# Last edge layer of a graph network: sums and expansions cut into pieces between the halves of the gathers, and four signals of TensorE for nine

## The chip, the cores and the metric

The kernel runs on one core of a Trainium2 chip. Its engines are TensorE (PE, matrix products into PSUM), VectorE (DVE), ScalarE (ACT), GpSimd (POOL, which issues the indirect DMAs here) and SyncE (SP, which issues the plain loads). The metric is the time of one execution on the device in microseconds.

## The reference, cut to what matters

A graph with 6250 nodes of 16 features and 206250 edges, sorted by their target node, goes through four graph layers. The change touches only the fourth, in which every edge has one of 90 relation types:

```python
def _L3_gnn_ref(h, he, Ws, Wa, weight, w_comp, src, dst, rel_type):
    W_rel = jnp.matmul(w_comp, V).reshape(num_rels, in_dim, out_dim)   # 90 matrices of 16 x 16
    h_src = h[src]
    e = jnp.concatenate([h_src @ Ws.T, he @ Ws.T, h[dst] @ Ws.T], axis=1) @ Wa.T
    msg = jnp.einsum('ei,eio->eo', h_src, W_rel[rel_type]) * e
    return jax.ops.segment_sum(msg, dst, num_segments=n_nodes)

h = jnp.maximum(_layernorm(x, axis=-1), 0.0)
x = x + _L3_gnn_ref(h, edge_attr_16, ..., src, dst, edge_type_90)
```

So each edge fetches its source node's row, multiplies it by the matrix of its type, weighs it by a scalar, and is added into its target's row.

## The kernel before, in words

`relation_layer` (from line 2043) does this layer in groups of 1024 edges: `SUP` = 8 tiles of 128 edges (`SE` = 1024), 202 groups k in all. A group is of one of three kinds (`kinds`). The first `PLAIN` = 11 are "plain": POOL fetches their source rows by indirect DMA, while TensorE makes a table with the product of every node and every type. The rest alternate nearly one to one. 96 are "table" groups: POOL fetches the finished products by indirect DMA (L2191, 8 per group, slots for `RT` = 12 groups). 95 are "matmul" groups: everything is computed on the engines. `EK` lists the plain and matmul groups, `GK` the table groups; iteration i of the loop stands for EK[i], and `after[i]` holds the table groups between it and the next.

The steps of a matmul group i:

- `make_hot` (L2194, DVE): after the keys were loaded by SP, 7 one-hot tiles of 1024 edges (L2206, L2207) and one of the types (`tyh`, L2211). Its buffer is one of two, so it waits for the last gather of group i - 2.
- `gather` (L2218, PE): for each half h of the edges (512) and each of two tables p, 7 matmuls of 128x512 into the PSUM bank `ps_g[p]` (L2225). Each set of seven gives a signal, and ACT evicts the bank with a relu into `sel` (L2231). The next set into the same bank waits for that eviction.
- `fold_rows` (L2233, PE): 16 small matmuls of 16 columns (L2240) turn the four `sel` tiles into the source rows in `ps_f`; they wait for the last eviction. `keep_rows` (ACT, L2248) copies them to `G`.
- `expand` (L2250, PE): 24 matmuls of 256 columns (L2260) put each edge's 16 x 16 matrix into the four banks `ps_w`; each bank waits for the product of the group before. Two signals, after 12 and after 24.
- `messages` (DVE): reads `G` (L2271), multiplies `ps_w` by `G` (L2288), reduces (L2280), and weighs (L2298). `make_dst` (L2216, DVE) makes the one-hots of the targets.
- `add_up` (L2306, PE): 8 fp32 products, 16 records in the profile (L2312), add a group's messages into a window of 64 nodes in one half of the bank `ps_a`. They wait for the messages and for the copy of the group two before. `put_sums` (ACT, L2323, L2326) copies the window out and stores it by DMA. A table group has the same two steps, after `weigh_rows` (L2303, L2304, DVE).

Iteration i issues, in this order for each engine: loads of keys (SP), fetches of table groups (POOL), `fold_rows(i-1)`, `keep_rows(i-1)`, `expand(i-1)`, the one-hots of i + 1 and the messages of i - 1 (DVE), both halves of `gather(i)`, `add_up` and `put_sums` of group EK[i-2], and the same for the table groups after it. Each engine works through its own list in order. The engines meet only through semaphores: `c.by(ins)` makes an instruction add to a counter and returns the value to wait for (L84). In a steady iteration TensorE gives 9 such signals: 4 of the gather, 1 of the fold, 2 of the expansion, 1 for each of the two sums. Who waits for the signal of a sum (`a_tok`): `put_sums` on ACT, `make_dst` and `messages` of a later group on DVE, and POOL, before it fetches the table group 12 later into the same slot. While plain groups run, one table tile (`table_tile`) stands in the middle of the expansion.

## Time and profile before

| | us |
|---|---|
| median of 3 runs | 4394.57 |
| lowest, highest | 4373.16, 4407.93 |
| profiled execution | 4357.18 |
| its span | 4353.5 |
| TensorE busy in the span | 3665.5 |

The span runs from the first to the last instruction of the program; the profiled execution is longer by what lies around it. The busy time of TensorE comes from matmuls that overlap and whose ends are modelled, so a busy TensorE isn't one at its peak. In the timeline, a row merges instructions of one kind; "idle before" is the time its engine stood, with what ended it. Names of tiles are shortened: `l_ps_g` is `ps_g`, `l_ps_x` is `ps_f` and `ps_a`, `ring` holds the one-hots, the products and the rows of table groups.

### The profile page before, as it was taken

The page shows a single profiled execution, that of the slowest core. Times are in us where ns is not written, and L with a number is a line of the kernel's source. Part 1 is how long each engine was busy: PE and PEld are TensorE (multiplying, and loading weights), DVE is VectorE, ACT ScalarE, POOL GpSimd, SP SyncE. Part 2 cuts the span into 40 slices and gives each one's busy share as a digit, 9 for nine tenths or more (in the row PEclk, how much of TensorE's full clock was granted, in tenths as well). Part 3 has the DMA queues.
Part 4 walks back from the last instruction along what each step waited for, and adds up shares of the span by engine and source line. Part 5 has one row for each costly group of instructions (what it writes and reads, how often), then busy time and mean ns, then how long its engine had stood idle before and what let it go on. Part 6 is the DMA issues. An engine that isn't in the chain of part 4 may idle for free. (4 is left out here: it accounts for less than half of the span.)

```text
span 4353.5 us, 77864 instructions
## 1 busy us (share of the span) xinstructions
PE 3665.5 (84%) x28548; PEld 2130.3 (49%) x28548; DVE 2710.6 (62%) x6415; ACT 1324.1 (30%) x2874; POOL 1900.8 (44%) x1856
## 2 busy tenths in 40 slices
PE   6787879999998768888889896672799989998998
PEld 4566645544554324444444443341455555555555
DVE  8999953222212546676666674442677767777777
ACT  6999930011000213332333331340122212222222
POOL 1000006830000466676667650267366666666650
PEclk8999989998999879898888997665799888888889
DMA  5444468662465412222222225771122222222221
GB/s 149 83 83 80 60 270 304 219 236 91 168 238 245 138 30 50 50 51 47 44 50 51 51 51 192 295 238 18 37 44 44 44 39 44 46 45 41 44 44 40
DMA packets 471195, 445.62 MB, mean 102 GB/s; under 512 B 357553, under 2 KB 406609, under 8 KB 459675
## 3 DMA queue, kind: packets, MB, share of 16 engines
q1 hardware_dynamic: 389178, 391.82, 29.1%
q0 software_dynamic: 55216, 38.70, 6.0%
q10 hardware_dynamic: 26417, 10.05, 0.9%
q8 instruction: 231, 3.78, 0.4%
q14 instruction: 153, 1.25, 0.1%
HBM read 346.18 MB, written 95.85 MB: 102 GB/s over the span
## 5 line engine op out<-in xcount | busy, mean ns | idle before, releaser
L1814 POOL DMA_INDIRECT rows<-typed_table,ring x640 | 754.4, 1179 | 368.1 <-issue 180.1
L2225 PE MATMUL l_ps_g<-ring,h_part 128*128 128x512 f16 x2660 | 641.8, 401 | 92.3 <-issue 81.3
L1408 PE MATMUL L_ps<-ring,L_T 128*128 128x448 fp8e4 (+1 forms) x4606 | 670.9, 382 | 45.6 <-DMA ring<-adj 42.1
L2191 POOL DMA_INDIRECT ring<-typed_table,l_idxA x384 | 397.1, 1034 | 275.8 <-PE l_ps_x L2312 163.9
L1408 PEld LDWEIGHTS L_ps<-ring,L_T 128*128 128x128 f16 (+1 forms) x4606 | 327.9, 104 | 375.8 <-issue 60.8
L2191 POOL DMA_INDIRECT l_rows<-typed_table,l_idxA x384 | 394.6, 1028 | 234.1 <-PE l_ps_x L2312 127.4
L2231 ACT ACTIVATE l_sel<-l_ps_g 128x512 f16<-128x512 f32 x380 | 226.1, 597 | 851.6 <-PE l_ps_g L2225 399.1
L2225 PEld LDWEIGHTS l_ps_g<-ring,h_part 128*128 128x128 f16 x2660 | 273.6, 103 | 431.4 <-issue 165.4
L620 PE MATMUL cells<-keys,lows 128*128 128x147 f16 (+5 forms) x2744 | 372.6, 283 | 121.6 <-DVE keys L581 105.9
L2206 DVE TENSOR_SCALAR ring<-l_krow,W 128x1024 f16<-128x1024 f16 x570 | 234.7, 483 | 302.9 <-remote 183.2
L2260 PE MATMUL l_ps_w<-rel,l_tyh 90*128 90x256 bf16 x2544 | 397.5, 327 | 19.1 <-DVE ring L2288 15.6
L1843 ACT ACTIVATE sel<-ps_g 128x512 f16<-128x512 f32 x488 | 263.3, 596 | 477.9 <-PE ps_g L1837 321.4
L1873 DVE TENSOR_TENSOR dinvB<-G,tyh 128x1024 f16<-128x1024 f16 x244 | 288.2, 1223 | 165.5 <-ACT G L1860 107.9
L1837 PE MATMUL ps_g<-ring_fifth,h_part 128*128 128x512 f16 x1464 | 365.8, 408 | 25.7 <-issue 25.0
L620 PEld LDWEIGHTS cells<-keys,lows 128*128 128x128 f16 x2744 | 286.7, 141 | 204.7 <-DVE keys L581 171.8
L1837 PE MATMUL ps_g<-dinvB,h_part 128*128 128x512 f16 x1464 | 370.0, 414 | 3.7 <-issue 3.3
L581 DVE TENSOR_SCALAR keys<-build_or_wx,offset 128x441 f16<-128x441 f16 (+3 forms) x1438 | 366.2, 332 | 0.0
L1420 DVE SCALAR_TENSOR_TENSOR L_Y<-L_ps,L_scale,dinvB 128x448 f32<-128x448 f32 x84 | 57.4, 684 | 493.9 <-PE L_ps L1408 493.6
L2260 PEld LDWEIGHTS l_ps_w<-rel,l_tyh 90*128 90x128 bf16 x2544 | 287.5, 116 | 100.4 <-issue 29.4
L698 ACT ACTIVATE ring<-cells 128x784 fp8e4<-128x784 f32 x392 | 326.1, 833 | 24.0 <-PE cells L620 23.6
L2288 DVE TENSOR_TENSOR ring<-l_ps_w,l_G 128x512 f32<-128x512 f32 x380 | 258.8, 683 | 46.0 <-remote 33.3
L2280 DVE TENSOR_REDUCE l_msg<-ring 128x32 f32<-128x512 f32 x424 | 278.3, 678 | 0.0
(369 smaller groups left out, 4466.4 us busy)
## 6 DMA issues: line engine op xcount, KB each, us to landing
ring<-adj SPq DMA_DIRECT2D x67, 2744.0 KB, 10.9
adj<-ring SPq DMA_DIRECT2D x14, 2744.0 KB, 9.1
typed_table<-ring SPq DMA_DIRECT2D x49, 765.0 KB
ring_fifth<-src_div_mod_rows SPq DMA_DIRECT2D x122, 256.0 KB
l_krow<-src_div_mod_rows SPq DMA_DIRECT2D x95, 256.0 KB
l_trow<-type_row SPq DMA_DIRECT2D x106, 180.0 KB
attr<-in_he POOLq DMA_DIRECT2D x25, 512.0 KB, 5.7
klast<-last_keys SPq DMA_DIRECT2D x81, 128.0 KB
```

What stands on the lines that cost most here:

```text
L581: ins = dve.tensor_scalar(keys[g % OB][:, j, 0:C], iotaC[:, 0:C], offset[g // BG % 2][:, g % BG, j:j + 1], HIT, ALU.is_equal, ALU.mult)
L620: ins = pe.matmul(to, lows[g // QG % 3][:, :, g % QG * KT + j], made[:, (a1 - a) * NT:(b1 - a) * NT], start=j == FIRST[h], stop=j == LAST[ ...
L698: act.activation(ring[c % RING][:, :, gl * GD:(gl + 1) * GD].rearrange("p k (h d) -> p k h d", h=2), cells[g % CB][:, :, 0:HD * NT].rearra ...
L1408: ins = pe.matmul(bank[at:at + rows, 0:CH], d["T"][q][:, k, 0:rows], ring[r][:, k, :], start=n < side, stop=n >= NT - side, tile_position= ...
L1814: r_tok_[g] = r_in[b].by(pool.indirect_dma_start(rows[b][:, j, :], None, t1_dram, bass.IndirectOffsetOnAxis(ap=idxA[:, k * SUP + j:k * SUP ...
L1837: ins = pe.matmul(ps_g[2 * h + p][:, 0:HE], parts[p][:, j, :], hot[b][:, j, h * HE:(h + 1) * HE], start=False, stop=j == GJ - 2)
L1843: selt[i, h] = c_sel.by(act.activation(sel[b][2 * h + p][:, :], ps_g[2 * h + p][:, 0:HE], ACT.Relu))
L1873: typed_tok[i] = c_typed.by(dve.tensor_tensor(typed[b][:, p, :, :, :], gp, ty, ALU.mult))
L2191: rt_tok[g] = r_in[b].by(pool.indirect_dma_start(table_rows[b][:, j, 0:RC], None, t3_dram, bass.IndirectOffsetOnAxis(ap=idxA[:, k * SUP + ...
L2225: ins = pe.matmul(ps_g[p][:, 0:HE], parts[p][:, j, :], hot[b][:, j, h * HE:(h + 1) * HE], start=j == 0, stop=j == GJ - 1)
L2260: ins = pe.matmul(ps_w[q][:, (j % 2) * 256:(j % 2 + 1) * 256], tyh[i % 3][:, j * P:(j + 1) * P], rel[:, p, :], start=p == 0, stop=p == 2)
L2280: return c_msg.by(dve.tensor_reduce(m[:, 2 * q:2 * q + 2, 0:F], prod[q], AX.X, ALU.add))
```

## The change

It moves work of the last layer on TensorE and lets tokens ride on other instructions' signals.

- `gather`: one signal for a half, after both banks; ACT waits once and evicts both.
- `expand` comes in two calls of 12 matmuls with one signal each; `fold_rows` stands between them and has no signal of its own: its token is that of the second half. `keep_rows` comes after it.
- `add_up` of the group EK[i-2] stands between the two halves of `gather(i)`; its token is that of the second half of the gather.
- The sums of the table groups stand after the gather as before, but have no signal; their token is that of the first half of the next iteration's expansion, and their `put_sums` comes there.

In iterations without a gather, and at the end, the sums keep signals of their own. A steady iteration has 4 signals of TensorE.

```diff
                         ins = pe.matmul(ps_g[p][:, 0:HE], parts[p][:, j, :], hot[b][:, j, h * HE:(h + 1) * HE],
                                         start=j == 0, stop=j == GJ - 1)
-                    gat[i, h] = c_gat.by(ins)
-                    act.wait_ge(*gat[i, h])
-                    if p == 0 and i >= 2 and by_matmul[i - 2]:
-                        act.wait_ge(*fold_tok[i - 2])
+                gat[i, h] = c_gat.by(ins)
+                act.wait_ge(*gat[i, h])
+                if i >= 2 and by_matmul[i - 2]:
+                    act.wait_ge(*fold_tok[i - 2])
+                for p in range(2):
                     selt[p, "sel"] = selt[i, h] = c_sel.by(act.activation(sel[b][2 * h + p][:, :], ps_g[p][:, 0:HE], ACT.Relu))
...
-                        ins = pe.matmul(ps_f[:, j * F:(j + 1) * F], sel[i % 2][2 * h + p][:, q * P:(q + 1) * P], fold[:, :], start=p == 0, stop=p == 1)
-                fold_tok[i] = c_fold.by(ins)
+                        pe.matmul(ps_f[:, j * F:(j + 1) * F], sel[i % 2][2 * h + p][:, q * P:(q + 1) * P], fold[:, :], start=p == 0, stop=p == 1)
...
-            def expand(i, between=()):
+            def expand(i, half):
                 pe.wait_ge(*ty_tok[i])
-                for q in range(SUP // 2):
-                    if q == SUP // 4:
-                        for m in between:
-                            table_tile(m)
+                for q in range(half * SUP // 4, (half + 1) * SUP // 4):
...
-                    if q % 2:
-                        w_tok[i, q - 1] = w_tok[i, q] = c_w.by(ins)
+                w_tok[i, q - 1] = w_tok[i, q] = c_w.by(ins)
+                if half == 1 and by_matmul[i]:
+                    fold_tok[i] = w_tok[i, q]
...
-                a_tok[k] = c_a.by(ins)
+                return ins
...
                 if 1 <= i <= n:
+                    expand(i - 1, 0)
+                    for k in unsignalled:
+                        a_tok[k] = w_tok[i - 1, 0]
+                        put_sums(k)
+                    unsignalled = []
                     if by_matmul[i - 1]:
                         fold_rows(i - 1)
+                    for m in tiles[ahead:ahead + 1]:
+                        table_tile(m)
+                    expand(i - 1, 1)
+                    if by_matmul[i - 1]:
                         keep_rows(i - 1)
-                    expand(i - 1, tiles[ahead:ahead + 1])
...
-                if i < n and by_matmul[i]:
+                gathers = i < n and by_matmul[i]
+                if gathers:
                     gather(i, 0)
+                if i >= 2:
+                    k = EK[i - 2]
+                    summed = add_up(k, dstP[(i - 2) % 3], msg[(i - 2) % 3], 2 * F, msg_tok[i - 2], dst_tok[i - 2])
+                if gathers:
                     gather(i, 1)
                 if i >= 2:
-                    k = EK[i - 2]
-                    add_up(k, dstP[(i - 2) % 3], msg[(i - 2) % 3], 2 * F, msg_tok[i - 2], dst_tok[i - 2])
+                    a_tok[k] = gat[i, 1] if gathers else c_a.by(summed)
                     put_sums(k)
                     for g in after[i - 2]:
                         k = GK[g]
-                        add_up(k, dstG[g % 4], table_rows[g % RT], MC, rows_tok[g], dstg_tok[g])
-                        put_sums(k)
+                        summed = add_up(k, dstG[g % 4], table_rows[g % RT], MC, rows_tok[g], dstg_tok[g])
+                        if i < n:
+                            unsignalled.append(k)
+                        else:
+                            a_tok[k] = c_a.by(summed)
+                            put_sums(k)
```

## Rows read from the trace of the kernel before

**Rows 1.** Page: busy time over the span, and the clock in 40 slices

```profile
PE 3665.5 (84%) x28548; PEld 2130.3 (49%) x28548; DVE 2710.6 (62%) x6415; ACT 1324.1 (30%) x2874; POOL 1900.8 (44%) x1856
...
PEclk8999989998999879898888997665799888888889
```

**Rows 2.** Windows: length, busy us (count) by engine, clock, DMA share, GB/s

```profile
3210.00:3320.00 110.00, 97.07 (x855) 60.98 (x852) 87.02 (x200) 26.70 (x60) 68.90 (x68) 1.00 0.23 44
...
4241.00:4338.00 97.00, 92.71 (x875) 62.28 (x873) 80.73 (x186) 25.38 (x61) 0.00 (x0) 0.98 0.10 24
3606.40:3621.70 15.30, 13.74 (x102) 8.51 (x101) 11.87 (x28) 3.05 (x7) 10.31 (x11) 0.84 0.34 56
3621.70:3633.60 11.90, 11.90 (x103) 7.42 (x101) 9.16 (x22) 3.05 (x7) 6.29 (x7) 0.92 0.21 32
...
3100.00:4338.00 1238.00, 1141.43 (x9194) 712.89 (x9192) 952.87 (x2184) 276.99 (x642) 697.31 (x672) 0.89 0.22 42
```

**Rows 3.** Timeline of PE, an iteration near the end: start, length, instructions

```profile
4261.85 6.21 PE L2225 MATMUL l_ps_g<-ring,h_part 128*128 128x512 f16 x28
4267.99 0.94 PE L2312 MATMUL l_ps_x<-l_msg,ring 128*64 128x32 f32 x13
...
4269.77 0.56 PE L2240 MATMUL l_ps_x<-fold,l_sel 128*128 128x16 f16 x16
4270.18 2.78 PE L2260 MATMUL l_ps_w<-rel,l_tyh 90*128 90x256 bf16 x24
4272.80 0.60 PE L2225 MATMUL l_ps_g<-ring,h_part 128*128 128x512 f16 x2
```

**Rows 4.** Timeline of ACT, the same iteration

```profile
4268.10 0.60 ACT L2231 ACTIVATE l_sel<-l_ps_g 128x512 f16<-128x512 f32 x1 [0.91 <-PE l_ps_g L2225]
...
4271.61 0.28 ACT L2248 ACTIVATE l_G<-l_ps_x 128x128 f32<-128x128 f32 x1 [0.78 <-ACT l_sums L2323]
```

**Rows 5.** Timeline of DVE, the same iteration

```profile
4267.48 0.29 DVE L2304 TENSOR_TENSOR ring<-ring,l_eG 128x128 f32<-128x128 f32 x1
4268.17 2.47 DVE L2206 TENSOR_SCALAR ring<-l_krow,W 128x1024 f16<-128x1024 f16 x6 [0.40 <-PE l_ps_g L2225]
...
4271.34 0.67 DVE L2216 TENSOR_TENSOR ring<-iota,dloc 128x512 f32<-128x512 f32 x1
4271.94 0.27 DVE L2271 TENSOR_TENSOR l_ua<-l_G,t_u 128x128 f32<-128x128 f32 x1
```

**Rows 6.** Timeline of PE, a long iteration in the middle

```profile
3606.41 6.21 PE L2225 MATMUL l_ps_g<-ring,h_part 128*128 128x512 f16 x28
...
3614.15 0.33 PE L2312 MATMUL l_ps_x<-ring 128*64 128x33 f32 x3 [0.22 <-issue]
3615.55 0.42 PE L2312 MATMUL l_ps_x<-ring 128*64 128x33 f32 x5 [1.06 <-issue]
3616.24 0.56 PE L2240 MATMUL l_ps_x<-fold,l_sel 128*128 128x16 f16 x16 [0.27 <-ACT l_sel L2231]
...
3616.66 5.28 PE L2260 MATMUL l_ps_w<-rel,l_tyh 90*128 90x256 bf16 x24
```

**Rows 7.** Timeline of ACT, the same long iteration

```profile
3608.13 0.60 ACT L2231 ACTIVATE l_sel<-l_ps_g 128x512 f16<-128x512 f32 x1 [2.61 <-PE l_ps_g L2225]
3609.64 0.60 ACT L2231 ACTIVATE l_sel<-l_ps_g 128x512 f16<-128x512 f32 x1 [0.91 <-issue]
3614.13 0.60 ACT L2231 ACTIVATE l_sel<-l_ps_g 128x512 f16<-128x512 f32 x1 [3.90 <-PE l_ps_g L2225]
3615.59 0.60 ACT L2231 ACTIVATE l_sel<-l_ps_g 128x512 f16<-128x512 f32 x1 [0.86 <-remote]
```

**Rows 8.** Groups of TensorE, 3100 to 4338: busy us, mean ns, idle before

```profile
L2240 PE MATMUL l_ps_x<-fold,l_sel 128*128 128x16 f16 x1456 | 53.3, 170 | 25.5 <-issue 15.6 <-ACT l_sel L2231 9.6
```

More of the change, by code:

```diff
@@ L2352, in relation_layer @@
                 if 1 <= i <= n:
+                    expand(i - 1, 0)
+                    for k in unsignalled:
+                        a_tok[k] = w_tok[i - 1, 0]
+                        put_sums(k)
+                    unsignalled = []
                     if by_matmul[i - 1]:
                         fold_rows(i - 1)
+                    for m in tiles[ahead:ahead + 1]:
+                        table_tile(m)
+                    expand(i - 1, 1)
+                    if by_matmul[i - 1]:
                         keep_rows(i - 1)
-                    expand(i - 1, tiles[ahead:ahead + 1])
                 if i >= 2:
```

## The prediction

> **What bounds it now.** I read the page first, then busy time by stretches, then the order of time on one engine at a time. The page's slices place the change: it touches only the last edge layer, about the last third of the span, where the clock row stays at 8 to 9 tenths for the most part [rows 1]. From 3100 to 4338 us, where gathers run, TensorE is busy 1141 of 1238 us and VectorE 953: TensorE is the bound, VectorE next, and POOL and ScalarE are not near [rows 2]. Count iterations by matmuls: one with gather, expansion, fold and both sums has 28 + 24 + 16 + 32 = 100 records, so 9194 are 92 iterations (the code has 95, the first of them earlier), 13.47 us each. An iteration at its best is seen near the end, when POOL has nothing more to fetch: from one gather's start to the next 4272.80 - 4261.85 = 10.95 us, without an idle gap [rows 3]. So 92 x (13.47 - 10.95) = 231 us of this layer are above its own best pace. Where they go is in a pair of neighbouring iterations that repeats (3606.4 to 3633.6): 15.3 us, then 11.9 us, at granted clocks of 0.84 and 0.92, that is, with some of the time at the 1.2 GHz level [rows 2].
>
> The long one shows how it is lost. The 28 gather matmuls take 6.21 us as they do at best [rows 3, 6]. But ScalarE, which should get one bank of four every 1.5 us (4268.10 is 6.25 after the gather's start) [rows 4], evicts the third at 3614.13, 7.7 us after the start, and the fourth at 3615.59, 9.2 us after it [rows 7]. The signals came about 3 us late. TensorE went on into the sums, then stood 0.22, 1.06 and, before the fold, 0.27 us for ScalarE [rows 6]; after that the expansion runs at half rate, 5.28 us for 24 against 2.78 [rows 3, 6]. The clock fell right after that idle. Near 3210 to 3320 the clock was full (1.00), yet 855 matmuls in 110 us are 12.87 us an iteration, so late signals cost without the clock falling too [rows 2]. No row tells why signals are late; with POOL idle (0.00 from 4241) they are not.
>
> **The change, part by part.** All sums are against the profiled execution, 4353.5 us of span and 4357.18 in all; the median of the three runs is 37.4 above that, and I add differences to the median.
>
> *Work on TensorE*: the same 100 matmuls, moved. Removed 0, added 0.
>
> *Nine signals to four* (four banks to two, fold, and both sums ride on others; two of the expansion stay). In the clean iteration the expansion's 24 matmuls with their two signals take 4272.80 - 4270.18 = 2.62 us, 109 ns each, and nothing stands behind a signal [rows 3]. Price 0; between 0 and, were a third of the 0.30 us of idle in front of such pieces due to signals, -9 us. I take 0. The Trainium skill (TensorE: Matmul & The Clock Gate, "The cost: per-tile semaphore tail") has increments that follow each other closely serialize at some 26 ns apiece; five fewer on 95 iterations would by that be an estimated 12 us, and the sum 12 us lower. The rows agree with none of it, as these signals lie microseconds apart.
>
> *More pieces.* Before: gather, two sums, fold, expansion. After: half expansion, fold, half expansion, half gather, sum, half gather, sum. 28 gathers at the pace inside the piece would be 6.04 us, and the sums start 6.14 after the gather did: a switch costs about 0.10 [rows 3]. There are up to three more per iteration: 0 to 0.30 us x 95 = 0 to +28; I take one, +10, since fold to expansion shows none.
>
> *Fold behind half an expansion.* Fold waits for ScalarE's last eviction. Over the layer TensorE stood 25.5 us before the fold, 9.6 of it put to ScalarE [rows 8]. Now the second sum and 12 expansion matmuls (1.3 us at full clock) run first, so that both evictions (2 x 0.60 after the signal) are covered even for a late signal. Gain 9.6 to 25.5; I take 20. What was late next in that place is nothing: the expansion waits for VectorE's products, done before.
>
> *Evictions after the pair.* The half's two relus start after 14 matmuls instead of 7 and 7. The next half's first bank needs the first relu, 0.03 + 0.60 us after the signal [rows 4]. The first sum, 16 of the 32 matmuls that take 1.78 us with their switch, about 0.9 us [rows 3], covers it with 0.3 us to spare. Price 0; without that cover 0.63 x 95 = +60.
>
> *ScalarE's and VectorE's order.* G is kept after the whole expansion instead of just after the fold, though before it stood behind two evictions of sums anyway: 4271.61, 1.84 us after the fold began [rows 3, 4]. Afterwards it comes at gather's end + 1.0 (switch and sum) + 2.6 + 0.4 (expansion, fold) + 0.3 and 0.3 (signal, the copy itself), so 4.6 us; VectorE is ready for it 3.8 us after it starts the one-hots at the gather's end (4268.17 to 4271.94) [rows 5]. So VectorE first stands 0.8 us. Its own work is 10.55 us of 10.95, with 0.40 of idle in front of the one-hots [rows 5]; it then starts its next round up to 0.4 us after the gather, finds G in time, and TensorE takes nothing from it sooner than a whole round later. Price 0, bound +0.4 x 95 = +38. At half clock G comes 2.5 us later still (5.28 against 2.78), but that pair gives VectorE 27.2 - 2 x 10.55 = 6 us of slack. The puts of sums and their DMAs are as many as before; the second sum's leaves ScalarE and frees POOL's slot half an expansion, some 1.3 us, later. POOL fetches 12 groups ahead, is busy 697 of 1238 us [rows 2] and waits for slots anyway: 0. SyncE's key loads and the plain part's table tiles keep their places: 0.
>
> Sum: +10 - 20 = -10 us, bounds -35 to +95 with every cover lost. 4394.57 - 10 = **4385**.
>
> **The rivals.** With a layer that has two regimes, these count for more than the sum.
>
> *A, the clock no longer falls.* The low-work stretch (two sums and fold, 2.2 us, lengthened by the idle) is cut up, so that the stretch of 3210 to 3320 becomes the rule: 92 x (13.47 - 12.87) = -55 us, 4340. For it: the clock fell right behind such a stretch [rows 6]. Against: 4241 to 4338 has the same uncut stretch at 0.98 clock, so the late signals, not the order, make it fall. 0.22.
>
> *B, the late signals go as well*, for fewer signals or a different rhythm: 10.95 + 0.15 us an iteration, 92 x 2.37 = -218, 4177. For it: such iterations exist; against it: those seen in number have an idle POOL, which the change doesn't give. 0.13.
>
> *C, slower: a late signal now hits between the halves.* The second half may not start before the first half's relu, and only 0.3 us is spare, where before every bank had the other bank's 1.5 us. If the signal of half 0 comes 3 us late, TensorE stands 2.7 us. If the lateness moves there, it replaces 0.22 + 1.06 + 0.27 = 1.55 us of idle [rows 6]: 46 long iterations x 1.15 = +53. If it comes at both, 46 x 2.7 = +124. Between them +88, 4483. It decides from 0.3 us of lateness on. For: between 3 us late evictions nothing in the trace binds them to the second half for good. Against: in the iteration read here the second is evicted at 3609.64, 3.2 us after the start, on time [rows 7]. 0.15.
>
> *D, slower: a fall in every iteration.* If the extra switches leave small gaps, the clock may fall each time, and every iteration takes 15.3: 92 x 1.83 = +168, 4563. The full clock from 4241 with four pieces speaks against it. 0.05. The Trainium skill has such a rule (TensorE: Matmul & The Clock Gate, "A second HAM failure mode: psum-queue depth-cycling"): short idles between groups of matmuls on cycling banks make the clock swing. What the trace has behind the 3616 idle agrees, the clean tail doesn't.
>
> *E, the change does nothing*, as when POOL or something outside paces the pair of iterations at 27.2 us: 4395. 0.05.
>
> **How the numbers follow.** The forecast has 0.40, spread 4350 to 4430. A measurement of this kernel tells about 1%, 44 us, from no change. Faster by more: A, B and little else, 0.36. Slower: C, D and an edge of the forecast with covers lost, 0.22. Within: 0.42. The range leaves out most of B and D, and reaches from between A and B to C: 4270 to 4485. The forecast's own range is 4350 to 4430.
>
> **What would show it.** In the profile after: (1) before the fold no idle on ScalarE, or this term is wrong; (2) from gather half to sum and back steps of 0.1 us; (3) ScalarE's relus in pairs, the first half's 0.03 us after its last matmul's end; (4) VectorE before L2271 up to 0.8 us idle and TensorE none for it; (5) long and short iterations alternating as before, 13.5 us on average: 12.9 says A, 11.1 B, over 14.3 C, 15.3 D. TensorE standing before the second half for ScalarE would make the prediction wrong upward, a granted clock above 0.95 downward.

## The result, and the profile after

The change made the kernel slower. Over 20 runs of each the median is 4414.43 us after (4366.08 to 4447.0) against 4374.65 before (4335.08 to 4413.82): a ratio of 1.0101, with an interval of 1.0072 to 1.0129, or some 44 us. (This ratio and those in the table below leave out executions more than 1.5% above the fastest of the same kernel, so they can differ a little from the ratio of the medians.) The forecast was 10 us faster; measured is 31 to 56 us slower. The time still lies inside the stated range, because that range reached far to both sides. The profiled execution took 4409.81 us with a span of 4405.7 (before 4357.18 and 4353.5).

In the changed kernel the gather is L2225 as before, its relu L2232, the fold L2241, the copy of G L2248, the expansion L2257, the sums L2310, their copies L2321, and the first read of G L2269. The page of the kernel after, first TensorE's clock, which hardly differs from [rows 1]:

```profile
PE 3665.5 (83%) x28548; PEld 2117.1 (48%) x28548; DVE 2716.7 (62%) x6415; ACT 1298.2 (29%) x2874; POOL 1905.9 (43%) x1856
...
PEclk8999989999998689889999997665998979998988
```

The same windows as in [rows 2], of after (window, its length, busy us and count of PE, PEld, DVE, ACT, POOL, granted clock, DMA share, GB/s):

```profile
3100.00:4380.00 1280.00, 1161.48 (x9217) 708.17 (x9214) 962.46 (x2196) 255.90 (x645) 709.94 (x672) 0.91 0.22 41
4285.00:4380.00 95.00, 94.11 (x844) 61.30 (x842) 81.33 (x185) 23.39 (x60) 0.00 (x0) 1.00 0.14 29
...
3200.00:4200.00 1000.00, 900.99 (x7079) 547.41 (x7078) 741.84 (x1694) 195.81 (x496) 611.75 (x578) 0.90 0.23 42
```

and the stretch 3200 to 4200 of before:

```profile
3200.00:4200.00 1000.00, 919.67 (x7301) 570.97 (x7300) 765.04 (x1753) 221.93 (x513) 619.74 (x598) 0.89 0.23 44
```

At 100 matmuls an iteration, 1000 us hold 73.01 iterations of before, 13.70 us each, and 70.79 of after, 14.13 us each. 0.43 us over the 95 iterations is 41 us, about the whole loss, at a clock that is no lower. (The two profiled executions differ by 52 us; from the layer's first expansion to its last matmul it is 43, and 8 lie before it, where nothing was changed.) Of the 0.43 us, 0.13 is more busy time of TensorE (12.60 against 12.73 us an iteration) and 0.30 is more idle time (1.10 against 1.40).

An iteration at its best, near the end where POOL is idle, shows the new order. The timeline of TensorE after (start, length, instructions):

```profile
4308.91 3.19 PE L2225 MATMUL l_ps_g<-ring,h_part 128*128 128x512 f16 x14
4312.02 1.12 PE L2310 MATMUL l_ps_x<-l_msg,ring 128*64 128x32 f32 x16
4313.07 3.19 PE L2225 MATMUL l_ps_g<-ring,h_part 128*128 128x512 f16 x14
4316.20 1.12 PE L2310 MATMUL l_ps_x<-ring 128*64 128x33 f32 x16
4317.25 1.48 PE L2257 MATMUL l_ps_w<-rel,l_tyh 90*128 90x256 bf16 x12
4318.57 0.55 PE L2241 MATMUL l_ps_x<-fold,l_sel 128*128 128x16 f16 x16
4318.98 1.47 PE L2257 MATMUL l_ps_w<-rel,l_tyh 90*128 90x256 bf16 x12
4320.28 1.89 PE L2225 MATMUL l_ps_g<-ring,h_part 128*128 128x512 f16 x8
```

From one gather to the next it is 4320.28 - 4308.91 = 11.37 us, without an idle gap, where before took 10.95 [rows 3]. By pieces, from start to start: gather 3.11 + 3.13 = 6.24 against 6.14 (+0.10); sums 1.05 + 1.05 = 2.10 against 1.78 (+0.32); expansion 1.32 + 1.30 = 2.62 against 2.62; fold 0.41 against 0.41. ScalarE and VectorE in the same iteration:

```profile
4312.13 1.09 ACT L2232 ACTIVATE l_sel<-l_ps_g 128x512 f16<-128x512 f32 x2 [2.75 <-PE l_ps_g L2225]
4316.31 1.09 ACT L2232 ACTIVATE l_sel<-l_ps_g 128x512 f16<-128x512 f32 x2 [3.09 <-PE l_ps_g L2225]
...
4320.48 0.28 ACT L2248 ACTIVATE l_G<-l_ps_x 128x128 f32<-128x128 f32 x1 [1.39 <-PE l_ps_w L2257]
```

```profile
4320.79 0.29 DVE L2269 TENSOR_TENSOR l_ua<-l_G,t_u 128x128 f32<-128x128 f32 x1 [0.57 <-ACT l_G L2248]
```

The relus come in pairs, and the second pair (4316.31) is done under the sum and half an expansion. VectorE stands 0.57 us for G, and nothing on TensorE waits for it.

In the middle of the layer the late signals are there as before ([rows 6, 7]). TensorE, ScalarE and VectorE in such an iteration of after:

```profile
3712.71 1.12 PE L2310 MATMUL l_ps_x<-l_msg,ring 128*64 128x32 f32 x16
3714.91 3.18 PE L2225 MATMUL l_ps_g<-ring,h_part 128*128 128x512 f16 x14 [1.08 <-issue]
3718.03 0.71 PE L2310 MATMUL l_ps_x<-l_rows,ring 128*64 128x33 f32 x9
3719.13 0.19 PE L2310 MATMUL l_ps_x<-l_rows,ring 128*64 128x33 f32 x1 [0.40 <-issue]
3719.84 0.53 PE L2310 MATMUL l_ps_x<-l_rows,ring 128*64 128x33 f32 x6 [0.52 <-issue]
```

```profile
3714.17 1.09 ACT L2232 ACTIVATE l_sel<-l_ps_g 128x512 f16<-128x512 f32 x2 [2.68 <-PE l_ps_g L2225]
3720.03 1.08 ACT L2232 ACTIVATE l_sel<-l_ps_g 128x512 f16<-128x512 f32 x2 [4.78 <-remote]
```

```profile
3720.11 2.46 DVE L2206 TENSOR_SCALAR ring<-l_krow,W 128x1024 f16<-128x1024 f16 x6 [1.80 <-remote]
```

The first half of this gather ended at 3712.8, its relu began 1.4 us later, and the second half of the gather began 1.08 us after the sum, at 3714.91, just behind the first relu (3714.17 + 0.60); the profile puts that idle to no wait. The second half ended at 3718.1 and its relus began at 3720.03.

A signal is "late" here against the end of a matmul, and those ends are modelled. What is late is on TensorE's side and not ScalarE's reception: VectorE, which waits for the same signal before it makes new one-hots, starts 0.08 us after ScalarE. In the long iteration of before it is the same, 3615.59 on ScalarE [rows 7] and on VectorE

```profile
3615.66 2.47 DVE L2206 TENSOR_SCALAR ring<-l_krow,W 128x1024 f16<-128x1024 f16 x6 [3.33 <-remote]
```

And TensorE itself stands inside a sum then, where the program has no wait between the 16 matmuls: 1.06 us in [rows 6], until 3615.55, and 0.40 and 0.52 us in the rows of after, until 3719.84. Whether its matmuls or only its signals are held up, and by what, no row tells. Counted over 3200 to 4200, VectorE waits 65 times before the one-hots in both kernels; 34 of these waits in before and 55 in after end more than 0.3 us behind the gather's last matmul, by 3.0 and 2.7 us in the median. So the change did not make late signals rarer.

Over the layer (3100 to 4380, groups of TensorE and one of VectorE: count, busy us, mean ns, idle before):

```profile
L2225 PE MATMUL l_ps_g<-ring,h_part 128*128 128x512 f16 x2561 | 640.0, 406 | 39.7 <-issue 33.5 <-ACT l_sel L2232 6.2
L2257 PE MATMUL l_ps_w<-rel,l_tyh 90*128 90x256 bf16 x2208 | 318.6, 298 | 19.5 <-issue 19.3
...
L2241 PE MATMUL l_ps_x<-fold,l_sel 128*128 128x16 f16 x1472 | 53.6, 171 | 39.9 <-ACT l_sel L2232 31.5 <-issue 8.2
```

```profile
L2269 DVE TENSOR_TENSOR l_ua<-l_G,t_u 128x128 f32<-128x128 f32 x92 | 26.8, 291 | 74.7 <-ACT l_G L2248 42.2 <-issue 32.5
```

The first and the last of them in before, 3100 to 4338:

```profile
L2225 PE MATMUL l_ps_g<-ring,h_part 128*128 128x512 f16 x2530 | 604.3, 398 | 23.1 <-issue 12.1 <-ACT l_sel L2231 11.0
```

```profile
L2271 DVE TENSOR_TENSOR l_ua<-l_G,t_u 128x128 f32<-128x128 f32 x91 | 25.4, 279 | 27.8 <-ACT l_G L2248 15.7 <-issue 11.9
```

The idle before the fold did not go away, it rose from 25.5 us [rows 8] to 39.9; that before the gathers rose from 23.1 to 39.7, and the expansion, which never stood before, stands 19.5 us. The sums stand less, 18.5 us for 46.7.

### The profile page after: what moved, and what is told of

The parts are those of the page before. It is cut to its first block and busy times, and to the rows that moved or that the text cites. A ratio compares the mean times of both kernels' runs of the same rounds, so it can differ in the third digit from the quotient of the medians.

```text
span 4405.7 us, 77969 instructions
## 1 busy us (share of the span) xinstructions
PE 3665.5 (83%) x28548; PEld 2117.1 (48%) x28548; DVE 2716.7 (62%) x6415; ACT 1298.2 (29%) x2874; POOL 1905.9 (43%) x1856
## 5 line engine op out<-in xcount | busy, mean ns | idle before, releaser
L2225 PE MATMUL l_ps_g<-ring,h_part 128*128 128x512 f16 x2660 | 671.1, 408 | 85.7 <-issue 79.1
L2225 PEld LDWEIGHTS l_ps_g<-ring,h_part 128*128 128x128 f16 x2660 | 269.1, 104 | 414.4 <-issue 172.2
L2232 ACT ACTIVATE l_sel<-l_ps_g 128x512 f16<-128x512 f32 x380 | 206.2, 595 | 845.5 <-remote 415.4
L2257 PE MATMUL l_ps_w<-rel,l_tyh 90*128 90x256 bf16 x2544 | 383.0, 306 | 47.6 <-issue 39.2
L1837 PE MATMUL ps_g<-ring_fifth,h_part 128*128 128x512 f16 x1464 | 356.2, 401 | 19.2 <-issue 18.5
L2257 PEld LDWEIGHTS l_ps_w<-rel,l_tyh 90*128 90x128 bf16 x2544 | 259.0, 108 | 120.6 <-issue 66.8
```

Of the source, the lines that this page charges most:

```text
L1837: ins = pe.matmul(ps_g[2 * h + p][:, 0:HE], parts[p][:, j, :], hot[b][:, j, h * HE:(h + 1) * HE], start=False, stop=j == GJ - 2)
L2225: ins = pe.matmul(ps_g[p][:, 0:HE], parts[p][:, j, :], hot[b][:, j, h * HE:(h + 1) * HE], start=j == 0, stop=j == GJ - 1)
L2257: ins = pe.matmul(ps_w[q][:, (j % 2) * 256:(j % 2 + 1) * 256], tyh[i % 3][:, j * P:(j + 1) * P], rel[:, p, :], start=p == 0, stop=p == 2)
```

## The experiments

Five groups ran, each on one chip beside runs of the kernel before. The chips turned out to be of two kinds. On chips 2 and 13 hardly a signal of TensorE comes late (none of 75 such waits in e1 and of 68 in e2, 3 of 71 in k0) and before takes about 3780 us; on chips 9, 14 and 4, and in the runs of the result above, about half of them or more come late, by 1.6 to 3.7 us in the median, and before takes 4375 to 4469. Each ratio is against before on the same chip; "us per iteration" is the window's length by its matmuls over 100 (900 us from 2800 on chips 2 and 13, else 1000 us from 3200).

| run | chip | median us | before | ratio (95%) | us per iteration | clock |
|---|---|---|---|---|---|---|
| e1_sum_between | 2 | 3797.64 | 3778.34 | 1.0056 (1.0034 to 1.0079) | 11.35 | 1.00 |
| e2_fold_between | 2 | 3784.66 | 3778.34 | 1.0011 (0.9988 to 1.0033) | 10.93 | 1.00 |
| e3_five_signals | 2 | 3848.83 | 3778.34 | 1.0190 (1.0154 to 1.0226) | 11.89 | 1.00 |
| e4_sums_together | 2 | 3847.17 | 3778.34 | 1.0183 (1.0150 to 1.0216) | 11.83 | 1.00 |
| a0_after | 9 | 4513.43 | 4468.78 | 1.0126 (1.0051 to 1.0200) | 14.70 | 0.89 |
| b0_before | 9 | 4445.18 | 4468.78 | 0.9950 (0.9899 to 1.0001) | 14.09 | 0.87 |
| e8_after_nine | 9 | 4382.99 | 4468.78 | 0.9833 (0.9766 to 0.9899) | 13.29 | 0.95 |
| e5_before_no_fetch | 9 | 4198.08 | 4468.78 | 0.9422 (0.9311 to 0.9533) | 11.46 | 0.99 |
| f1_gather_signals | 14 | 4388.40 | 4392.16 | 0.9987 (0.9944 to 1.0031) | 14.04 | 0.90 |
| f2_other_signals | 14 | 4321.21 | 4392.16 | 0.9852 (0.9794 to 0.9911) | 13.27 | 0.96 |
| g1_fold_between | 14 | 4374.65 | 4392.16 | 0.9969 (0.9932 to 1.0005) | 13.67 | 0.90 |
| g2_sum_between | 14 | 4363.01 | 4392.16 | 0.9957 (0.9921 to 0.9993) | 13.68 | 0.91 |
| k0_after | 13 | 3798.09 | 3781.07 | 1.0052 (1.0031 to 1.0073) | 11.36 | 1.00 |
| k1_sum_signals | 13 | 3798.09 | 3781.07 | 1.0051 (1.0027 to 1.0075) | 11.37 | 1.00 |
| k2_fold_signal | 13 | 3790.62 | 3781.07 | 1.0042 (1.0016 to 1.0067) | 11.36 | 1.00 |
| k3_pool_later | 13 | 3794.63 | 3781.07 | 1.0035 (1.0014 to 1.0056) | 11.35 | 1.00 |
| m1_sum_signals | 4 | 4465.06 | 4462.62 | 0.9979 (0.9940 to 1.0018) | 14.13 | 0.92 |
| m3_pool_later | 4 | 4446.97 | 4462.62 | 0.9964 (0.9932 to 0.9997) | 13.97 | 0.91 |

### One part of the order at a time

**e1_sum_between** is the kernel before, with its nine signals, and only the sum of EK[i-2] moved between the halves of the gather.

```diff
                 if i < n and by_matmul[i]:
                     gather(i, 0)
-                    gather(i, 1)
                 if i >= 2:
                     add_up(k, dstP[(i - 2) % 3], msg[(i - 2) % 3], ...)
+                if i < n and by_matmul[i]:
+                    gather(i, 1)
```

> Of the change only this: the sum of group EK[i-2] stands between the two halves of the gather; fold, expansion and all nine signals as before. Theory S (switches): in the kernel after, an iteration at its best takes 11.38 us instead of 10.95, all of it because two sums that stood together took 1.78 us and now take 1.05 each, and the gather in two pieces takes 6.25 instead of 6.14. Then this kernel has a best iteration of 11.38 us too, and costs 92 x 0.43 = +40 us, about as much as the whole change (+1.0%). Theory L (late signals): what costs is that TensorE stands more for ScalarE, mostly before the fold, which here is where it was; then this is +0 to +15 us. Theory N (number of signals matters): nine signals kept, the switches' cost without the gain from fewer signals, over +1.0%.

**e2_fold_between** is the kernel before with only the fold moved between the halves of the expansion.

```diff
+                    expand(i - 1, 0)
                     if by_matmul[i - 1]:
                         fold_rows(i - 1)
                         keep_rows(i - 1)
-                    expand(i - 1, tiles[ahead:ahead + 1])
+                    for m in tiles[ahead:ahead + 1]:
+                        table_tile(m)
+                    expand(i - 1, 1)
```

> Of the change only this: the fold stands between the two halves of the expansion, with its own signal, and G is kept right after it. Theory S: a piece of expansion more costs nothing (1.32 + 0.40 + 1.31 us in the kernel after against 0.41 + 2.62), best iteration 10.95, and the fold's idle of 25.5 us goes mostly: 0 to -20 us, no difference that can be told. Theory L: the idle before the fold grows as in the kernel after (39.9 us), +10 to +20 us.

The windows 2800 to 3700, of e1 and then of e2:

```profile
2800.00:3700.00 900.00, 900.00 (x7930) 580.97 (x7928) 827.91 (x1901) 240.94 (x555) 706.88 (x634) 1.00 0.28 53
```

```profile
2800.00:3700.00 900.00, 900.00 (x8237) 586.94 (x8236) 863.23 (x1976) 250.79 (x577) 700.68 (x655) 1.00 0.29 54
```

No idle in either, at full clock; e2 keeps the pace of before (10.93 against the 10.95 of [rows 3]), e1 is at 11.35. In the iteration Theory S holds: moving the one sum costs all of the 0.42 us, the split expansion nothing. Where it lies, on TensorE of e1 and of e2:

```profile
3306.90 3.19 PE L2225 MATMUL l_ps_g<-ring,h_part 128*128 128x512 f16 x14
3310.02 1.12 PE L2312 MATMUL l_ps_x<-l_msg,ring 128*64 128x32 f32 x16
3311.07 1.25 PE L2225 MATMUL l_ps_g<-ring,h_part 128*128 128x512 f16 x5
```

```profile
3309.04 0.94 PE L2309 MATMUL l_ps_x<-l_msg,ring 128*64 128x32 f32 x13
3309.76 0.24 PE L2309 MATMUL l_ps_x<-ring 128*64 128x33 f32 x1
...
3309.96 0.92 PE L2309 MATMUL l_ps_x<-ring 128*64 128x33 f32 x13
3310.82 1.38 PE L2257 MATMUL l_ps_w<-rel,l_tyh 90*128 90x256 bf16 x11
```

Side by side the sums run 13 matmuls in 0.72 us (55 ns each), then six records that alternate between the two in 0.20 us (33 ns each), then 13 in 0.86. Alone, 16 take 1.05 us. At 55 ns each 16 would be 0.89, so the end of a sum costs some 0.16 us, now twice, and the six that overlapped lose 6 x 22 ns = 0.13: 0.29 of the 0.32. The other 0.10 is the second start of a gather (14 x 216 ns = 3.02 of the 3.12 that a half takes). The Trainium skill (TensorE: Matmul & The Clock Gate, "Measured speedup vs the span model") has matmuls on different column tiles run in parallel, three of them 2.38 times as fast. Here two tiles (the two halves of `ps_a`) overlap only where the second sum follows the first, in six records of 32.

The whole program lost less than these iterations say: by medians e1 lost 19 us, not 0.42 x 95 = 40, and k0 below 17. In the two profiled executions the stretch from the first gather to the last is 43 us longer in e1 than in e2, but the median of e2 lies some 16 us above its profiled execution. Runs of before spread over 41 us, those of e1 over 16. Why the typical run of before and of e2 is slower than its own best pace there is open.

### Signals where none is late

**e3_five_signals** is the order of before with merged signals: one for each half of the gather, one for the two sums, the fold's on the expansion's. **e4_sums_together** is the kernel after with the plain sum moved back behind the gather, next to the table sum; both tokens are then that of the next half expansion.

```diff
# e3, against before
-                    gat[i, h] = c_gat.by(ins)
+                gat[i, h] = c_gat.by(ins)
...
-                fold_tok[i] = c_fold.by(ins)
+                        fold_tok[i - 1] = w_tok[i - 1, 0]
# e4, against after
                     gather(i, 0)
+                    gather(i, 1)
                 if i >= 2:
                     summed = add_up(k, dstP[(i - 2) % 3], ...)
-                if gathers:
-                    gather(i, 1)
```

> Order of the kernel before, but five signals for nine: one per half of the gather with both evictions behind it, the fold's token is that of the first half of the expansion, and two sums that stand together share one. Theory S: signals cost nothing, best iteration 10.95, within 0.3% of before. Theory N: fewer signals come late less often, mean iteration under 13.2 us, -20 us or more. Theory L: evictions in pairs make the next half wait for the relu (no sum covers it here): each iteration +0.63 us, best iteration 11.6, +58 us.

> The kernel after with one thing undone: the sum of EK[i-2] stands behind the whole gather again, next to the table group's sum, and both tokens are that of the next half expansion (4 signals). But now nothing covers the first relu between the halves: 0.63 us. Theory S: the sums take 1.78 together again and the gather 6.14; less 0.43 and, if the cover matters as I reckoned, plus 0.6: best iteration 11.0 if the relu is covered by something else, 11.6 if not. Total 0 us or +58 us against before. Theory L: as the kernel after, +44 us, whatever the order of the sums.

TensorE in e3:

```profile
3306.96 3.18 PE L2225 MATMUL l_ps_g<-ring,h_part 128*128 128x512 f16 x14 [0.78 <-ACT l_sel L2232]
```

Every second half stands 0.78 us for the relu of the first, 74.0 us in all, and e4 shows the same 0.78. Both lose 1.8 to 1.9%, about 70 us: that is the price of the pair of relus without its cover, which the prediction put at +60. In after the sum covers it, for 0.42 us.

**k0_after** is the changed kernel itself, **k1_sum_signals** gives the sums their signals back, **k2_fold_signal** the fold its own, and **k3_pool_later** has all nine, but POOL waits for the later token that it has in the changed kernel.

```diff
# k1, against after (add_up; put_sums again right behind it)
-                return ins
+                a_tok[k] = c_a.by(ins)
# k2, against after (fold_rows)
+                fold_tok[i] = c_fold.by(ins)
# k3, against the nine signals of e8 below
-                    pool.wait_ge(*a_tok[GK[g - RT]])
+                    at = next(x for x in range(n) if g - RT in after[x])
+                    pool.wait_ge(*w_tok[at + 2, 0])
```

> The kernel after, unchanged, as the measure for the three beside it on the same chip. With late signals +1.0 to +1.3% against before, without them +0.6 to +1.1%.

> The kernel after with both sums signalling for themselves again; the fold without a signal, the gather in pairs: six signals. Theory M1 (the sums' borrowed tokens cost, for the copies of sums and POOL's next fetch come later): as fast as with nine signals, 1.5% under before where signals come late. Theory M2 (the fold's borrowed token costs, for G comes half an expansion later): as the kernel after, +1%. Without late signals all three are within 0.3% of each other.

> The kernel after with the fold signalling for itself again; sums without signals, the gather in pairs: five signals. Theory M1: as the kernel after, +1%. Theory M2: 1.5% under before.

> The order of the kernel after with all nine signals (1.7% under before on a chip with late signals), but POOL waits for its free slot on the signal that it has in the kernel after, the next iteration's first half expansion, instead of the sum's own, some 1.4 us later. Theory Q (it is POOL's start, and where its fetches then fall on the gather, that makes the borrowed tokens costly): as slow as the kernel after, +1%. Rival A (it is ScalarE's copies of the sums, which come later or stand before G): stays 1.7% under before.

The window of k0:

```profile
2800.00:3700.00 900.00, 899.28 (x7924) 580.50 (x7923) 831.77 (x1901) 219.98 (x555) 707.30 (x633) 1.00 0.27 52
```

With four signals TensorE stood 0.72 us of 900, with nine (k3) not at all; all four kernels take 11.35 to 11.37 us an iteration, and their ratios lie within 0.17 points of each other, with intervals that overlap. Where hardly a signal is late, four or nine of them are the same, and the loss is that of the pieces alone. VectorE stands 46.5 us for G in these 900 us of k0, and TensorE has no idle for it.

### Where signals are late

**a0_after** and **b0_before** are the two kernels as they are, **e8_after_nine** is the order of after with every signal of before, and **e5_before_no_fetch** is the kernel before without POOL's fetches from the 13th table group on: their sums use the rows that lie in the slots.

```diff
# e8, against after
-                gat[i, h] = c_gat.by(ins)
+                    gat[i, h] = c_gat.by(ins)
...
+                fold_tok[i] = c_fold.by(ins)
...
-                return ins
+                a_tok[k] = c_a.by(ins)
# e5, against before
+                if g >= RT:
+                    rt_tok[g] = rt_tok[g - RT]
+                    return
```

> The kernel after, unchanged, beside the kernel before on whatever chip this is. Where the four kernels so far ran, no signal came late and each had one iteration time: 11.40 us with the sum between the halves, 10.94 with the fold between. Theory S (switches and the sums' lost overlap, 0.43 us an iteration): on a chip without late signals this kernel has 11.38 us in nearly every iteration, and is 20 to 43 us slower than before. On a chip with late signals both have 13 to 14 us and the same difference. Theory L (more idle for late signals): without late signals there is no difference.

> The kernel before, unchanged, to have its profile from the same chip. Theory S: 10.95 us in nearly every iteration if no signal comes late there; the last layer then ends some 240 us earlier after its first gather than in the trace of before. If the signals are late, 13.5 us as in the trace of before.

> The order of the kernel after with all nine signals of the kernel before (each bank of the gather, the fold and both sums signal for themselves, evictions per bank, G kept as after, behind the whole expansion). Theory S: signals cost nothing, iteration 11.38 to 11.40 us and the time of the kernel after within 0.3%. Theory N (five signals fewer gain something, 0.13 us an iteration or more): 11.5 us or more, 12 us slower than after.

> The kernel before without POOL's fetches for the table groups from the thirteenth on (their sums use the rows that lie in the slots), so that POOL is idle in most of the layer. Theory P (late signals come with POOL's fetches): on a chip where before has late signals, this one has none and 10.95 us an iteration. Rival (late signals are a state of the chip and of the load on TensorE alone): 13 us and more there too. On a chip without late signals both are 10.95.

The windows 3200 to 4200 of a0, b0, e8 and e5, in this order:

```profile
3200.00:4200.00 1000.00, 875.88 (x6805) 527.91 (x6803) 717.92 (x1638) 188.63 (x478) 592.65 (x562) 0.89 0.23 41
```

```profile
3200.00:4200.00 1000.00, 915.41 (x7097) 560.75 (x7096) 745.25 (x1707) 214.38 (x496) 604.92 (x584) 0.87 0.24 43
```

```profile
3200.00:4200.00 1000.00, 910.24 (x7527) 560.94 (x7526) 785.13 (x1806) 225.95 (x526) 665.37 (x616) 0.95 0.25 45
```

```profile
3200.00:4200.00 1000.00, 950.72 (x8725) 622.30 (x8723) 910.14 (x2091) 264.21 (x610) 0.00 (x0) 0.99 0.19 46
```

Three readings. Without the fetches the same program on the same chip goes from 14.09 to 11.46 us an iteration with a clock of 0.99, and late waits of VectorE go from 33 of 65 to 1 of 68: the late signals come with POOL's fetches (two executions of e5). Whether it is POOL's work or the traffic of its indirect DMAs is not told apart, and the same fetches do no harm on chips 2 and 13. The order alone, with nine signals, is a gain of 1.7% here (0.9766 to 0.9899): the clock rises from 0.87 to 0.95. It does not make the signals punctual, 61 of 71 waits are late in e8; it has work to do meanwhile. And merging the signals turns that into a loss of 1.3%: e8 to a0 is 4382.99 to 4513.43, 130 us or 3.0%. Theory S, the same +0.43 us as elsewhere (here a0 has +0.61 over b0) and e8 within 0.3% of after, failed. b0 is before against itself; its 0.5% says how much of a ratio on this chip is noise.

**f1_gather_signals** gives the changed kernel back only the four gather signals (six in all), **f2_other_signals** only those of the fold and the sums (seven), with the relus still in pairs. **g1_fold_between** and **g2_sum_between** are the edits of e2 and e1.

```diff
# f1, against after
-                gat[i, h] = c_gat.by(ins)
+                    gat[i, h] = c_gat.by(ins)
# f2, against after
+                fold_tok[i] = c_fold.by(ins)
...
-                return ins
+                a_tok[k] = c_a.by(ins)
```

> The kernel after with its gather signals undone: one signal and one eviction per bank (four again), while the fold and both sums still have none of their own; six signals. On the chip where signals come late, the kernel after took 14.5 us an iteration and its order with all nine signals 13.2. Theory E (evictions in pairs lengthen the path of a late signal: the fold then waits for two relus, 0.6 us more, and what the gather does next finds no bank free): this is as fast as with nine, 1.7% under before and 2.9% under after. Theory M (the merged tokens of fold and sums cost, as G, the copies of sums and POOL wait for a later signal): as the kernel after, +1%. On a chip without late signals both say +0.6 to +1.0% (11.38 us an iteration).

> The other half of it: the kernel after with signals of their own for the fold and both sums again, but one signal and paired evictions for each half of the gather; seven signals. Theory E: as slow as the kernel after, +1%. Theory M: as fast as with nine, 1.7% under before. Without late signals both +0.6 to +1.0%.

> The kernel before with only the fold between the halves of the expansion, nine signals, gather and sums whole, once more, hoping for a chip with late signals (on the one without it was 10.94 us an iteration, +0.1%). Theory C (what saved time in the order with nine signals is that work stands between the last, late eviction and the fold that needs it): a late signal is covered by half an expansion, 1.3 us: 92 x 0.6 to 1.3 = 55 to 120 us under before. Rival H (what saved it is the sum between the halves, which keeps the gather's halves apart): same as before.

> The kernel before with only the first sum between the halves of the gather, nine signals, once more (11.40 us an iteration and +0.56% on the chip without late signals). Theory C: the fold stands one sum closer to the gather's end, so a late signal is covered less: +0.43 + up to 0.9 us an iteration, +1 to +2.5%. Rival H: -1% or more where signals come late.

The windows of f1 and f2:

```profile
3200.00:4200.00 1000.00, 918.05 (x7125) 558.58 (x7124) 747.90 (x1708) 209.36 (x498) 612.43 (x584) 0.90 0.23 43
```

```profile
3200.00:4200.00 1000.00, 905.02 (x7533) 556.04 (x7531) 788.78 (x1806) 208.88 (x527) 661.13 (x616) 0.96 0.24 45
```

f2 is at the pace of e8 (13.27 and 13.29), as Theory M said. f1 is not (14.04), but it is not as slow as after either: its ratio lies 1.35 points above f2, on the same chip, and 1.1 to 1.4 points under those of after (1.0101 and 1.0126), so neither Theory E nor M has it. With the fold's and the sums' tokens on time, pairing the relus costs next to nothing. The merged tokens of fold and sums cost about half of what merging all costs, and the pairs the other half, on top of them.

Groups of TensorE, 3200 to 4200, of g1 and then of g2:

```profile
L2225 PE MATMUL l_ps_g<-ring,h_part 128*128 128x512 f16 x2044 | 495.3, 401 | 57.5 <-issue 40.7 <-ACT l_sel L2231 16.8
...
L2240 PE MATMUL l_ps_x<-fold,l_sel 128*128 128x16 f16 x1168 | 41.6, 172 | 0.0
```

```profile
L2225 PE MATMUL l_ps_g<-ring,h_part 128*128 128x512 f16 x2033 | 485.0, 392 | 1.9 <-ACT l_sel L2231 1.0 <-issue 0.9
...
L2240 PE MATMUL l_ps_x<-fold,l_sel 128*128 128x16 f16 x1168 | 41.2, 171 | 77.8 <-ACT l_sel L2231 77.8
```

In g1 the fold, behind half an expansion, never stands; the idle is before the gathers instead, 57.5 us. In g2 the gathers never stand, covered by the sum, and the fold does, 77.8. By their ratios each alone gains 0.3 to 0.4%, which is no more than b0 differed from itself and far from what either theory gave, with the idle moved to the place that is still uncovered; both together gain 1.5% on the same chip (f2) and 1.7% on chip 9 (e8).

**m1_sum_signals** and **m3_pool_later** are the edits of k1 and k3 on a chip with late signals.

> The kernel after with both sums signalling for themselves again (fold without a signal, gather in pairs), once more, for a chip with late signals. There the kernel after is at +1.0 to +1.3% against before, and with the fold's signal too it was at -1.5%. Theory M1 (the sums' borrowed tokens cost): -1% or less. Theory M2 (the fold's): +1%. Without late signals: +0.5% as last time, and nothing is told.

> The order of the kernel after with nine signals, POOL alone waiting for the later one, once more, for a chip with late signals. Theory Q (POOL's later start is what costs): +1%, like the kernel after, where the same kernel with POOL's own signal was at -1.7%. Rival A (not POOL's start): -1.7%. Without late signals: +0.35% as last time.

Their windows:

```profile
3200.00:4200.00 1000.00, 875.72 (x7076) 532.97 (x7075) 744.92 (x1701) 196.23 (x495) 619.21 (x580) 0.92 0.22 42
```

```profile
3200.00:4200.00 1000.00, 907.63 (x7157) 554.52 (x7155) 746.89 (x1717) 211.55 (x500) 617.61 (x588) 0.91 0.22 43
```

m3 has the order and the signals of e8, and only POOL's fetches begin half an expansion later; it gains 0.4% (0.9932 to 0.9997) where e8 gained 1.7%, so neither Q nor A has it. The wait for that later token is in the trace of after, on POOL:

```profile
3708.32 1.25 POOL L2191 DMA_INDIRECT l_rows<-typed_table,l_idxA  x1 [3.46 <-PE l_ps_w L2257]
```

So POOL's later start alone costs some 1.3 points. How is open: it fetches 12 table groups ahead, and VectorE, which weighs its rows, never stands for them (0.0 us in m3). That its fetches then fall on other work of TensorE was argued, not shown.

m1 (-0.2%) has neither M1's -1% nor M2's +1%. It differs from f2 in the fold's token alone and lies 1.3 points above it (0.9979 and 0.9852), so that token costs as well, at least with paired relus. VectorE before its first read of G, 3200 to 4200, in f2 and then in m1:

```profile
L2268 DVE TENSOR_TENSOR l_ua<-l_G,t_u 128x128 f32<-128x128 f32 x75 | 21.5, 286 | 10.5 <-issue 9.6 <-ACT l_G L2249 0.5
```

```profile
L2269 DVE TENSOR_TENSOR l_ua<-l_G,t_u 128x128 f32<-128x128 f32 x71 | 20.7, 292 | 66.0 <-issue 38.4 <-ACT l_G L2248 27.6
```

Wherever the fold's token is merged VectorE stands like this (54 to 70 us in the two traces of after, 69.3 in f1), and 7 to 12 us in the new order where it is not (e8, f2, m3). That this is what costs isn't shown, as TensorE shows no idle put to VectorE, and k0 has the same wait at no cost.

Against e8 the parts don't add up: pairs alone 0.2 points (f2), POOL's start alone 1.3 (m3), the fold's token with pairs 1.5 (m1), fold and sums without pairs 1.5 (f1), all together 2.9 (a0). Only the last of these is on one chip, the others are across chips (9, 14 and 4), and the split is no firmer than that.

## Why the prediction was wrong

The sign was wrong, -10 for +44. The two steps that failed most are the merged tokens, priced at 0, and the fold's cover, priced at -20; the pieces were priced too low.

*More pieces: +10, bound +28. Failed, in size.* I took one switch of 0.10 us. One at the gather was right. The other stood between the two sums, and the prediction priced a switch only by the gather's row, though the sums' own rows [rows 3] show that 32 of them take 1.78 us together. They measured +0.32: 0.42 an iteration in all. Over 95 iterations that is +40 us, above the bound I gave; the whole program lost only 17 to 19 us by medians (k0, e1), and why is open.

*Nine signals to four: 0. Failed where signals are late, and it is the larger error.* Where hardly one is late it is right: k0 to k3 have ratios within 0.17 points. On chip 9 it is +130 us. I weighed what a signal costs TensorE, and did not ask what each token that rides on a later instruction holds back while the signals are already late: POOL's next fetches, which I wrote down as 1.3 us later and "0", and the fold's token on ScalarE and so G on VectorE. That POOL waits for slots anyway was no reason: an engine that waits for a token starts later by as much as the token comes later (m3: 1.3 points). The Trainium skill's cost of increments (TensorE: Matmul & The Clock Gate, "The cost: per-tile semaphore tail"), by which five fewer would have gained an estimated 12 us, shows nowhere: nine and four are equal on chip 13.

*Fold behind half an expansion: -20. Failed for the changed kernel.* The prediction had both evictions covered "even for a late signal". By its own rows they aren't: a signal 3 us late and two relus of 0.60 are 4.2 us, and the second sum and half an expansion are 1.05 + 1.32 = 2.4. In after both relus of the second half wait for the one late signal, and the idle before the fold is 39.9 us where it was 25.5. The cover works when the relus come one by one behind a whole gather (g1: 0.0 idle before the fold), but the next place then stands. "What was late next in that place is nothing" looked at the fold only.

*A misreading.* The prediction has TensorE standing 0.22, 1.06 and 0.27 us for ScalarE. [rows 6] puts only the 0.27 to ScalarE; the others lie inside a sum, where TensorE waits for nobody. So the lateness isn't ScalarE's, and a change of ScalarE's order can cover it at best.

*Put together.* On chip 9: e8 against before is -75 us by its ratio, merged signals +130, sum +55, which is a0 against before (1.26% of 4469) by construction. If the pieces cost 20 to 40 us there as on chips 2 and 13, the cover of late signals gains an estimated 95 to 115. For the runs of the forecast, where signals are late too, this is the likely split, but only its sum, +44, was measured, with 0.30 us of idle and 0.13 us of busy time an iteration. That 0.43 us is also close to what the pieces cost alone (0.42) is then a coincidence of larger terms. That the time came out inside the range is luck in the same sense: a gain and a loss, each larger than the forecast's terms, nearly cancelled.

*The bound +95.* The sum's own terms give 28 + 60 + 38 - 9.6 = +116, or +126 with the fold's gain lost too.

*Evictions in pairs: 0 with cover, +60 without.* Right: nothing waits in the clean iteration, and 70 us without it (e3, e4).

*ScalarE's and VectorE's order: 0.* Right in the clean iteration, where VectorE stands 0.57 us (0.8 expected) and k0 loses nothing by it. Over the layer it stands 74.7 us (27.8 before), and TensorE shows no idle put to it; but the fold's later token, by which G comes later, costs 1.3 points in m1 against f2, so 0 is not shown where signals are late.

*Rivals.* A, the clock no longer falls (-55): its mechanism is real and appears in e8 and f2, at 0.95 and 0.96 and 13.3 us an iteration, but not with the merged signals (0.90). B, late signals go: refuted, 55 of 65 waits are late in after; they come with POOL's fetches (e5), which the change keeps. C, late signals between the halves (+88): seen in single iterations, as the 1.08 us at 3714.91, and the idle before the gathers is 39.7 us of after against 23.1 of before in its layer window; 17 us, not 88, and likely part of the +130. D, a fall in every iteration: refuted, the clock is not lower, and 1.00 near the end.

*What would show it.* The first sign, idle before the fold, said that this term is wrong. Steps of 0.1 us held at the gather and not at the sums. The first half's relu came 0.03 us after its last matmul's modelled end on chip 13 and in the tail (4312.10 and 4312.13), as said. Iterations long and short stayed, less regular than before; their mean is 14.1, between the forecast's 13.5 and C's 14.3.

The best kernels found are e8, the new order with every signal kept, 1.7% faster where signals are late, and f2, the same with paired relus, 1.5%. k3, the near twin of e8, suggests that e8 would be some 0.4% slower where they are not.

## What to carry to other kernels

Price a merged signal by what waits for its token, on every queue, and not by what the increment costs the engine that gives it: here five increments were free and the later tokens cost up to 3%. Before a run of like instructions is cut apart, look in its own rows for records that interleave, since the overlap goes with the cut. Add up what a cover must cover, here 4.2 us by 2.4. And when a stall is covered, name the next uncovered place: covering one of two gained at most 0.3 to 0.4%, both 1.5 to 1.7%.

## What the runs showed of the hardware

- The same kernel takes 3778 and 3781 us on two chips and 4375 to 4469 on the others. In the iterations of this layer the difference is some 3 us (14.09 on chip 9, 10.93 for e2 on chip 2), about 300 us. Most of the rest lies before the layer: its first expansion starts at 2860 us in b0 and at 2577 in e2. Why signals are late, and on some chips only, is open; that they come with POOL's fetches is shown on chip 9 alone.
- A late signal is late for ScalarE and VectorE alike (3615.59 and 3615.66; in after 3720.03 and 3720.11), and TensorE stands at the same time inside a run of matmuls that has no wait.
- On the chips without late signals the granted clock of this layer is 1.00, on the others 0.87 to 0.96; without fetches it is 0.99 on chip 9 too. In [rows 6] the fall follows the stalls.
- Two fp32 sums into different column halves of a bank take 1.78 us back to back, and 2 x 1.05 apart.
